# Graph layer on one core: the four one-hot chunks of a window summed on VectorE, and one degree product per window

## The reference

```
msg = (h[src] + edge_feats) @ Wn.T
agg = segment_sum(msg, dst) / max(deg, 1)
h   = leaky(agg + where(deg == 0, h @ Wi.T, h @ Ws.T))     # twice, with Wn0.. and Wn1..
out = layernorm(x + h)
```

## Time and profile before

| | |
|---|---|
| median of 3 executions | 1078.83 us (1078.09 to 1083.72) |
| the profiled execution: its time | 1072.14 us |
| its span, first to last instruction | 1070.3 us |
| TensorE busy | 942.5 us (88%) |
| VectorE busy | 696.6 us (65%) |
| ScalarE busy | 534.1 us (50%) |
| GpSimd busy | 756.2 us (71%) |
| mean granted TensorE clock | 0.962 of 2.4 GHz |

### The profile page before, as it was taken

The page is one execution under the profiler, slowest core; times in us unless marked ns, Lnnn a source line. Parts: engine busy times, 40 slices in busy tenths (PEclk is TensorE's granted clock), DMA queues, the critical chain, the costliest instruction groups (busy, mean ns, idle before and its releaser), DMA issues.

```text
span 1070.3 us, 38440 instructions
## 1 busy us (share of the span) xinstructions
PE 942.5 (88%) x14592; PEld 880.3 (82%) x14592; DVE 696.6 (65%) x2388; ACT 534.1 (50%) x1143; POOL 756.2 (71%) x757
## 2 busy tenths in 40 slices
PE   1599899989899798998979987989899989999994
PEld 0499888978799687888878877989889989999994
DVE  8868776876778767887677782355455545554334
ACT  7456565655566555765656661353245525533200
POOL 8367767777777777777777671777767767767671
PEclk9999999999999989999999977999999999999998
DMA  9467777877788758877877777767656856676772
GB/s 306 158 214 248 256 252 240 264 259 233 244 283 277 255 169 268 285 241 255 261 220 230 242 243 241 238 172 218 177 157 171 236 157 168 170 222 168 206 217 60
DMA packets 141368, 237.75 MB, mean 222 GB/s; under 512 B 20050, under 2 KB 101308, under 8 KB 138620
## 3 DMA queue, kind: packets, MB, share of 16 engines
q1 hardware_dynamic: 80832, 144.35, 41.2%
q0 software_dynamic: 35584, 72.92, 25.1%
q10 hardware_dynamic: 24764, 17.95, 5.4%
HBM read 182.71 MB, written 52.43 MB: 220 GB/s over the span
## 4 chain that ended last, share of the span: by engine, by line
PE 45%; POOL 8%; issue 6%; DVE 4%; DMA 3%; ACT 3%; ACTq 2%; SPq 1%; DVEq 0%; POOLq 0%
PE ps_dense L1341 16%; PE ps_count L1341 11%; POOL rows L577 8%; PE ps_count L1329 6%; PE ps_win L1280 6%; PE ps_self L1399 3%; DMA rows<-x_parts_rows,idx 2%; ACT counts L1127 2%; PE ps_node L1412 2%; DMA h_parts<-h_parts_rows 1%; DVE h_rest L926 1%; SPq L498 1%; ACTq L1102 1%; PE ps_win L1287 1%; PE ps_count L1333 1%
## 5 line engine op out<-in xcount | busy, mean ns | idle before, releaser
L1127 ACT CAST counts<-ps_count 128x294 f32 x992 | 456.8, 502 | 346.0 <-PE ps_count L1329 207.4
L577 POOL DMA_INDIRECT rows<-x_parts_rows,idx x442 | 446.8, 1011 | 158.1 <-issue 125.0
L1341 PE MATMUL ps_dense<-counts,h_parts 128*128 128x136 bf16 x5292 | 450.3, 226 | 11.4 <-DVE sums L825 7.2
L1341 PEld LDWEIGHTS ps_dense<-counts,h_parts 128*128 128x128 bf16 x5292 | 350.6, 99 | 44.8 <-issue 9.2
L577 POOL DMA_INDIRECT rows<-h_parts_rows,idx x286 | 279.3, 977 | 127.6 <-issue 86.0
L1329 PE MATMUL ps_count<-is_code,is_lane 128*128 128x294 bf16 x992 | 285.5, 312 | 31.9 <-ACT counts L1127 27.2
L1280 PE MATMUL ps_win<-onehot,feats 128*128 128x40 f32 (+1 forms) x1564 | 253.4, 241 | 33.7 <-DMA rows<-x_parts_rows,idx 13.3
L1280 PEld LDWEIGHTS ps_win<-onehot,feats 128*128 128x128 f32 (+1 forms) x1564 | 212.7, 163 | 40.1 <-issue 25.5
L790 DVE TENSOR_SCALAR is_lane<-column,lane 128x128 bf16<-128x128 bf16 x496 | 138.4, 279 | 99.9 <-PE ps_count L1333 91.4
L792 DVE TENSOR_SCALAR is_code<-codes,code 128x637 bf16<-128x637 f16 x496 | 198.6, 400 | 0.0
L1280 PE MATMUL ps_win<-onehot,rows 128*128 128x40 bf16 (+1 forms) x2224 | 150.4, 187 | 2.3 <-DVE sums L803 2.3
(11 more groups left out here) (99 smaller groups left out, 790.6 us busy)
## 6 DMA issues: line engine op xcount, KB each, us to landing
feats<-in_edges_dram SPq DMA_DIRECT2D x196, 256.0 KB
counts_kept<-counts SPq DMA_DIRECT2D x20, 1764.0 KB
counts<-counts_kept SPq DMA_DIRECT2D x140, 252.0 KB
rows<-x_parts_rows,idx POOLq DMA_INDIRECT x442
x_parts_rows<-h_parts SPq DMA_DIRECT2D x7, 672.0 KB, 8.0
h_parts<-h_parts_rows SPq DMA_DIRECT2D x7, 672.0 KB, 8.7
h_parts_rows<-row_parts ACTq DMA_DIRECT2D x16, 288.0 KB
rows<-h_parts_rows,idx POOLq DMA_INDIRECT x286
```

The source lines that it names most:

```text
L577: nc.gpsimd.indirect_dma_start(rows[:, SUB * slot + c, :], None, table[:, :], bass.IndirectOffsetOnAxis(ap=indices[:, c:c + 1], axis=0)).t ...
L1127: nc.scalar.copy(counts[:, buffer_of(j), :, at(offset + first, count)], ps_count[:, COUNT_BANK[q], 0:count * TILES].rearrange("p (r t) -> ...
L1341: last = nc.tensor.matmul(bank, h_parts[:, t, k, :], counts[:, b, t, 0:WIDE], start=(t == 0 and k == 0), stop=(t == TILES - 1 and k == PAR ...
```

## The change

A buffer `hot_sum` of one 128 x 40 fp32 matrix per window of the ring is added. After the one-hots of a window, VectorE sums its four matrices into it with one reduction over a transposed view. In layer 0 TensorE then makes a single degree product from it, behind a wait for the new semaphore, where it made four (two in the last window). `sum_degrees` stays for the path that doesn't run.

```diff
+        hot_sum = sb("hot_sum", [P, HOT, W])
...
+        hot_summed = sem("hot_summed")
...
+            def sum_hot(n):
+
+                h = SUB * (n % HOT)
+                dve.wait_ge(onehot_ready, n + 1)
+                nc.vector.tensor_reduce(hot_sum[:, n % HOT, :],
+                                        onehot[:, h:h + SUB, :].rearrange("p c w -> p w c"),
+                                        AX.X, ALU.add).then_inc(hot_summed, 1)
...
             def layer0():
                 for n in range(HOT):
                     make_onehot(n)
+                for n in range(HOT):
+                    sum_hot(n)
                 for n in range(AHEAD):
                     make_codes(n)
...
                     if k + 2 in SPLIT_OF:
                         split_feats(k + 2)
+                    if 1 <= k and k - 1 + HOT < WINDOWS:
+                        sum_hot(k - 1 + HOT)
                     if k in READY[0]:
...
                 if c == chunks_in(n) - 1:
                     if layer == 0:
-                        last = sum_degrees(ps_win[n % 2], onehot[:, SUB * (n % HOT):SUB * (n % HOT + 1), :], W, c + 1)
+                        pe.wait_ge(hot_summed, n + 1)
+                        last = nc.tensor.matmul(ps_win[n % 2][:, 0, DEG * W:(DEG + 1) * W], ones16[:, :],
+                                                upper(hot_sum[:, n % HOT, :]), start=True, stop=True)
                     last.then_inc(window_summed, 1)
```

## The result

The changed kernel takes 1093.27 us (median of 3, 1091.04 to 1102.84) against 1078.83: a ratio of 1.0156, 95% interval 1.0108 to 1.0204. It is slower, and 1093.27 lies above the forecast range. The profiled execution of the kernel before is one of its faster ones (1072.14 us; the median of 23 later executions was 1077.09), so the spans differ by 21.2 us where the medians differ by 14.4. What follows reads shapes and places from the two traces; how much a part costs is read from the timed runs.

What follows compares the result with a forecast made beforehand. GpSimd's gathers were taken to pace layer 0 from 156 to 598 us, TensorE counting only where GpSimd waits for it. Terms of -0.4, +0.3 and -0.6 gave -0.7 us: 1078.8 to 1078.1 us, range 1068 to 1090.

Steps and rivals of the forecast that it cites:

- 586 products removed, 14.7 us of TensorE: Layer 0, TensorE: 782 degree products become 196, saving 0.025 us each, 14.7 us, mostly turning into waiting for rows.
- The reduction, 0.24 us of VectorE's queue: Layer 0, VectorE: 196 reductions at 0.24 us plus 118 waits at 0.1 us, 59 us in all.
- The cover is twice the need on average: VectorE, 60 to 650 us: usable idle time of 120 us, 0.63 us per window, against 0.24 or 0.34 needed.
- each such wait of today grows by that lateness: TensorE's existing waits for VectorE's window and group adds each grow by VectorE's mean lateness, 0.4 us.
- twelve waits by 0.4 us: Waits for VectorE in three stretches of layer 0: 3, 5 and 4, adding 1.2, 2.0 and 1.6 us.
- The map of where TensorE's time counts: Layer 0: TensorE's time counts only up to 156, 236 to 308 and 560 to 650 us; elsewhere savings become waiting.
- The start, +1.0 us: Start of layer 0: four reductions of 0.24 us stand before the first codes, adding 1.0 us to the path.
- Gathers at an unchanged length: GpSimd, layer 0: gathers stay at 1.01 us, no term; slower gathers named only as something not seen.
- VectorE sets the pace: Rival: TensorE held at VectorE's window and group adds, 0.1 us per window, +14 us to 1093; chance of slower 0.25.
- the one on the cover: Sign of being wrong on VectorE's cover: TensorE's waits for the two adds grow by more than 10 us.

Runs made afterwards that it cites:

- the reductions of the middle stretch alone: Kernel before with VectorE's reductions added only for windows 44 to 166, four degree products kept and the sums unused: ratio 1.009.
- three of the milder forms: Changed kernel with reduction behind codes, 1.0106; two-half addition and two products instead, 1.008; that addition behind codes, add's columns loaded a beat earlier, 1.0021.

## Why the prediction was wrong

Forecast 1078.1 us, within 0.5% of before; measured 1093.27. By its steps:

- **586 products removed, 14.7 us of TensorE: right**, and so was that they are worth almost nothing (0.9965 alone). That they gain nothing at all is not excluded, as the interval ends at 1.0. Their price of 25 ns holds for this view only: 72 ns with a step of 16 bytes.
- **The reduction, 0.24 us of VectorE's queue: too low.** It is 0.33. I took the row of equal element count and kept the strided view as an upper bound of 0.5. With the wait it is 196 x 0.33 + 118 x 0.1 = 76 us instead of 59, and VectorE's busy time grew by 70.8 us where some 55 were forecast.
- **"The cover is twice the need on average", and "each such wait of today grows by that lateness", twelve waits by 0.4 us: this is the step that failed.** The lateness was about right, the number of waits was not. The mean wait for an add went from 15.8 / 18 = 0.88 to 36.6 / 31 = 1.18 us, 0.3 us more; over the old 18 that is 5.4 us. The other 15.4 us are 13 waits more than there were. For these 20.8 us GpSimd's idle time before its gathers grew by 15.2. I let only the waits of the trace grow. A window whose add came 0.2 us in time, say, has no row, and becomes a wait as soon as VectorE is 0.3 us later. VectorE's slack of 0.63 us per window was an average too: its waits for counted chunks, which were to take up the work, gave back 27.2 us (56.5 to 29.3) and not 55. That they came at other beats than the adds that were due is my reading; no row here shows it beat by beat.
- **The map of where TensorE's time counts: right for its small gain, wrong for a loss.** GpSimd's longest waits after are at the predicted places, 161, 311 and 623 us (5.6, 7.3 and 3.0 us for 2.68, 1.41 and 2.72). But the reductions of the middle stretch alone cost 0.9%, in their trace about half by GpSimd's idle time and half by longer gathers. A saving there turns into waiting for rows; a delay there is not absorbed in the same way, because the rows are held by slots that TensorE frees. Where two engines run at nearly the same pace, either one's delay is the path.
- **What a wait costs afterwards: missing.** 4.1 us of idle time were followed by 4 us at 1.2 GHz. No term stood for it. It isn't needed for a loss: the reductions of the middle alone cost 0.9% at an unchanged mean clock.
- **The start, +1.0 us: right.** The first gather that waits for a slot starts 1.3 us later (51.80 for 50.53).
- **Gathers at an unchanged length: a term put at nothing, off by 13 ns each**, 6.0 us of the 21.2 between the traces, with the mechanism open. It was named as what I hadn't seen. In the changed kernel it is the smaller part, in three of the milder forms the whole (the table above).

The rival "VectorE sets the pace" had the mechanism, the place (the two adds) and, at 1093, the size: it put 0.1 us per window, and the waits grew by 20.8 us over some 187 windows, 0.11 each. It got 0.25 because I asked whether the reduction uses up the mean slack; that was the wrong condition. That its number came out to the microsecond is luck: the 0.1 us was taken and not worked out, and part of the loss is longer gathers, which it didn't have. Of my signs for being wrong, the one on the cover came true: the waits for the two adds grew by more than 10 us.

## What to carry to other kernels

When work moves to a second engine, don't multiply the waits that the trace shows; count the hand-overs (here two adds per window or group) and ask how early each one is, since those without a row are the ones that turn up. A mean slack of twice the need is no cover if three engines run within a few per cent of each other: half the cost came through in the stretch that a third engine seemed to pace. And the same change gained 3.5% as soon as TensorE was plainly the slow one (and the products removed cost three times as much), so first ask by how much the relieved engine is the bound, not whether it is the busiest. Then look at the third engine's own instructions: gathers that were 1.5 to 2% longer make up the whole loss in the traces of three milder forms.

## What the runs showed of the hardware

- A bf16 moving operand read with a step of 16 bytes instead of 4 slows products of 40 columns from 25 to 72 ns apart, and cost 11% of this kernel. fp32 products of 40 columns hardly slowed (0.38 us for two instead of 0.36). The Trainium skill (SBUF — State Buffer, section Door 1: The DMA port swizzle) says that SBUF has lines of 16 bytes and that each access in a new line pays. The trace agrees for the bf16 products; the page gives no size. I had not weighed it.
- A reduction over every 40th fp32 element takes 0.332 us from start to start, over neighbouring ones 0.227, for 160 elements. It would fit the same rule; no run separates this from another cost of the view.
- A gather on GpSimd took 0.95 us beside reductions of the setup and 1.70 to 1.79 us, once 2.38, beside VectorE's additions and subtractions of two SBUF operands there. The Trainium skill (SBUF — State Buffer, section Who interferes with whom) says that a reduction never contends with GpSimd, which agrees, and infers that an addition of two tensors doesn't stall the making of descriptors, which these rows contradict.
- A wait of TensorE can cost it its clock: 4.1 us idle, behind a stall of VectorE of 4.9 us, were followed by 4 us at 1.2 GHz.
- The load of seven columns into registers stalled VectorE in front of the add for 30.5 us in 17 times, up to 4.9 us, and moving it one beat earlier moved the stall with it.
